# Products of zeros on TensorE through the whole routing, in counts per step

## The reference, cut to what matters

```
x = x + 0.5 * ffn(layernorm(x))
x = x + attention(layernorm(x))        # 16 heads of 16, causal
x = x + 0.5 * ffn(layernorm(x))

ffn(x):
    logits = x @ gate_w + gate_b                     # 8 experts
    probs = softmax(logits, axis=1)                  # over the 4096 tokens
    vals, idx = top_k(probs, 2)                      # 2 experts for each token
    y = relu(relu(relu(x @ w1[e] + b1[e]) @ w2[e] + b2[e]) @ w3[e] + b3[e])
    v[e] = sum over tokens of y[e] * (probs of e where e was chosen, else 0)
    out[token] = sum of v[e] over its 2 chosen experts
```

## Time and profile before

| | us |
|---|---|
| median of 3 runs | 2117.75 |
| lowest and highest | 2114.55, 2118.36 |
| the profiled execution's own time | 2126.23 |
| its span, first to last instruction | 2124.5 |
| TensorE busy / VectorE busy / ScalarE busy | 2047.7 / 1817.7 / 1598.6 |
| mean granted clock of TensorE, as a share of full | 0.975 |

### The profile page before, as it was taken

How to read it: one execution, slowest core, us unless ns; L and a number is a source line. 1 busy time by engine, 2 the same in 40 slices (tenths; PEclk the granted TensorE clock), 3 DMA queues, 4 the chain that set the end, 5 groups by cost and what they waited for, 6 DMA issues and landing times.

```text
span 2124.5 us, 99858 instructions
## 1 busy us (share of the span) xinstructions
PE 2047.7 (96%) x43659; PEld 1584.0 (75%) x43659; DVE 1817.7 (86%) x4023; ACT 1598.6 (75%) x3311; POOL 414.5 (20%) x1118
## 2 busy tenths in 40 slices
PE   5899989999999999999999999999999999879998
PEld 3788866377877777777787777777778776658885
DVE  6666666899999999999999999999999994676665
ACT  5344446599999999999999999999999998334442
POOL 1333213411121111121111111111111111023330
PEclk8899989999999999999999999999999999979998
DMA  8211103300010000100001001000010002231112
GB/s 273 74 47 50 42 16 125 134 30 25 13 34 14 25 30 8 34 20 18 31 7 33 22 16 34 9 29 27 11 34 16 22 4 69 54 118 47 45 49 88
DMA packets 70394, 94.36 MB, mean 44 GB/s; under 512 B 16640, under 2 KB 59396, under 8 KB 69956
## 3 DMA queue, kind: packets, MB, share of 16 engines
q1 hardware_dynamic: 62796, 68.75, 10.1%
q0 software_dynamic: 6816, 19.20, 3.4%
q10 hardware_dynamic: 344, 0.01, 0.0%
HBM read 62.24 MB, written 25.43 MB: 41 GB/s over the span
## 4 chain that ended last, share of the span: by engine, by line
PE 88%; DVE 6%; issue 2%; ACT 1%; POOL 1%; DMA 1%; SPq 1%; another core or an unknown queue 0%; DVEq 0%; ACTq 0%; POOLq 0%
PE bank L1264 39%; PE bank L1257 22%; PE bank L1139 17%; PE bank L1346 3%; PE bank L1150 1%; PE bank L1375 1%; DVE stats L1405 1%; PE bank L1307 1%; PE bank L1157 1%; DVE rows L1427 1%; DVE x_res L1725 1%; SPq L698 0%; POOL work L591 0%; DVE work L1594 0%; PE bank L1217 0%
## 5 line engine op out<-in xcount | busy, mean ns | idle before, releaser
L966 ACT ACTIVATE feat<-bank 128x512 f32<-128x512 f32 (+3 forms) x2304 | 1263.2, 565 | 113.8 <-PE bank L1264 13.3
L1264 PE MATMUL bank<-work 96*32 96x512 bf16 (+2 forms) x15872 | 1206.4, 370 | 5.0 <-DVE work L1772 3.8
L1772 DVE TENSOR_REDUCE work<-bank 128x1 f32<-128x512 f32 (+1 forms) x1920 | 1178.9, 659 | 26.4 <-PE bank L1264 23.4
L1257 PE MATMUL bank<-feat,phase 128*17 128x128 f32 (+3 forms) x18432 | 879.2, 263 | 0.3 <-ACT feat L972 0.3
L1257 PEld LDWEIGHTS bank<-feat,phase 128*17 128x17 f32 x18432 | 588.4, 98 | 270.7 <-ACT feat L972 13.7
L1264 PEld LDWEIGHTS bank<-work 96*32 96x32 bf16 (+1 forms) x15872 | 472.6, 96 | 57.1 <-DVE work L1772 24.6
L1139 PE MATMUL bank<-work 128*128 128x256 f32 (+1 forms) x1872 | 398.4, 363 | 0.6 <-issue 0.2
L1139 PEld LDWEIGHTS bank<-work 128*128 128x128 f32 x1872 | 325.1, 192 | 37.1 <-issue 1.0
L625 POOL TENSOR_SCALAR_AFFINE_SELECT feat<-feat 128x128 f32<-128x128 f32 x512 | 145.1, 292 | 456.0 <-ACT feat L966 439.1
L1656 DVE COPY work<-phase 128x514 f32 x234 | 101.5, 436 | 124.1 <-ACT work L880 99.5
L578 POOL DMA_INDIRECT work<-token_table,row_no x142 | 138.1, 973 | 299.0 <-PE bank L1150 142.6
(11 more groups left out here) (201 smaller groups left out, 1371.9 us busy)
## 6 DMA issues: line engine op xcount, KB each, us to landing
phase<-in_w SPq DMA_DIRECT2D x12, 1024.0 KB, 12.0
work<-qk_parts SPq DMA_DIRECT2D x60, 192.0 KB
token_table<-rows SPq DMA_DIRECT2D x8, 1056.0 KB, 8.7
work<-work SPq DMA_DIRECT2D x512, 0.5 KB
qk_parts<-phase SPq DMA_DIRECT2D x20, 384.0 KB, 2.8
work<-qk_parts SPq DMA_DIRECT2D x60, 128.0 KB
qk_parts<-work SPq DMA_DIRECT2D x12, 384.0 KB, 2.8
x_res<-in_x SPq DMA_DIRECT2D x8, 512.0 KB
```

What stands on the lines that cost most here:

```text
L966: eng.activation(p_ring[:, n % P_RING, lo:QB], s_bank("probs", n)[:, lo:QB], ACT.Exp, scale=HD ** -0.5).then_inc(sig.s_done, 1)
L1257: mm = eng.matmul(bank[ACC_BANK][GRID * g:GRID * g + VW, GRID * i0:P], v_aug[:, t, h, :], weights[:, i0:TPJ, g, :], start=(t == 0), stop=( ...
L1264: mm = eng.matmul(out[GRID * g:GRID * (g + 1), width], left[:, GRID * g:GRID * (g + 1)], right, start=start, stop=stop)
L1772: eng.tensor_reduce(maxima[:, h % 2, j, PLACE[i], at:at + 1], scores[:, 0:hi - lo], AX_X, ALU.max).then_inc(sig.a_done, 1)
```

## The change

A table gives the number of products of zeros for each step, and there are now some after the steps behind the counts, beside the first batch of one-hot columns (3 when its first instruction is done, 5 when its second is), and 3 ahead of each further batch of one-hot products. The five at the tiles' start stay as they were. The step `col_max` has none any more. Only TensorE's program is changed.

```diff
+BESIDE_CHOICE = {"pad": 2, "shifted": 6, "col_sum": 3, "inv_sum": 1, "probs": 2, "max_so_far0": 3, "from_top0": 2, "sel0": 2,
+                 "rest": 2, "max_so_far1": 3, "from_top1": 2, "sel1": 2}
+BESIDE_COUNTS = {"rounded": 1, "full": 1, "expert_rest": 1, "full_sum": 1, "over_half": 1, "left": 1, "others": 1}
+BESIDE_SLOTS = {"position": 2, "beyond": 2, "beyond_slots": 2, "slots": 2, "all_slots": 2, "my_slots": 3, "slots_of": 3,
+                "digits_hi": 1, "digits_lo": 1}
+BESIDE_HOTS = (3, 5)
+BETWEEN_HOTS = 3
...
+            def product_of_zeros():
+                eng.matmul(bank[4][:, :], zeros_bf[:, 0:P], zeros_bf[:, :], start=True, stop=True)
+
             def busy_beside(f, steps):
 
-                for name in steps:
+                for name, count in steps.items():
                     need.wait_ge(sig.routed[f], ROUTED[name])
-                    eng.matmul(bank[4][:, :], zeros_bf[:, 0:P], zeros_bf[:, :], start=True, stop=True)
+                    for _ in range(count):
+                        product_of_zeros()
 
             def route(f):
...
-                busy_beside(f, ROUTE[:ROUTE.index(FIRST_CHOSEN)])
+                busy_beside(f, BESIDE_CHOICE)
...
                 eng.matmul(bank[6][:, 0:NT * E], ones_bf[:, :], by_expert, start=True, stop=True).then_inc(sig.counted[f], 1)
+                busy_beside(f, BESIDE_COUNTS)
                 chosen_rows(f, 0, NT // 8)
+                busy_beside(f, BESIDE_SLOTS)
+                for made, count in enumerate(BESIDE_HOTS):
+                    need.wait_ge(sig.hots[f], made + 1)
+                    for _ in range(count):
+                        product_of_zeros()
                 for b in range(TOP * NT):
+                    if b and b % HOTS == 0:
+                        for _ in range(BETWEEN_HOTS):
+                            product_of_zeros()
                     need.wait_ge(sig.hots[f], 3 * (b // HOTS + 1))
...
             def tiles(f):
-                busy_beside(f, ["row_no"] * GATHER_FILL)
+                busy_beside(f, {"row_no": GATHER_FILL})
```

## The result

| | before | after |
|---|---|---|
| median, both on the same chip, 22 runs each (us) | 2117.53 (2113.92 to 2120.91) | 2120.67 (2118.80 to 2124.76) |
| the profiled execution, its span (us) | 2126.23, 2124.5 | 2121.85, 2120.1 |
| mean granted clock | 0.975 | 0.984 |

The ratio is 1.0018, 95% interval [1.0011, 1.0025]: by it the change is 3.8 us slower, where 2.3 us faster was forecast (the two medians as they stand are 3.1 us apart). 2120.67 lies just above the range. The clock did come up, and the kernel got slower.

What follows compares the result with a forecast made beforehand. It took VectorE's steps to bound the routings, with at most a few microseconds of 2117.75 hanging on TensorE's clock there. Gains of 1.17 us per routing, 2.3 in all, other terms 0, gave 2115.4 us; range 2112.0 to 2120.6.

Steps and rivals of the forecast that it cites:

- What bounds the kernel now: Routings' chain is mostly VectorE's; TensorE's clock matters at zeros, counts and last 16 one-hot products, at most a few microseconds.
- One-hot products: Last batch of each routing ends at 63.78 against 64.95 us: 1.17 us gained, with 0.5 from the counts.
- p: Time from one one-hot product to the next: 0.137 us at half clock, taken as 0.10 at full.
- Count products: Ahead of `running`: counts start 0.14 us later but shorten at full clock; gain 0.5 us, at worst a loss of 3.4.
- The loads do not quicken: Rival at the one-hot products: 0.137 us each even at full clock, +0.93 us x 2, 2119.6 us; chance 0.20.
- Does the clock stay up?: In the routings: full clock holds through the choice; a fall would mend itself as zeros queue at 0.43 us each.
- The clock falls among the one-hot products: Rival at 55 to 62 us: a batch takes 3.47 us, 2.9 us lost per routing, 2123.5 us; chance 0.10.
- Slots: Zeros behind the counts (7) and beside VectorE's slot steps (18): nothing on the chain waits, 0 us.
- Tiles' start: At the gather's wait the fill ends early, about 1 us idle; cost between 0 and 0.9 us, taken as 0.
- More is won at the tiles' start: Rival at the first tiles: both routings escape half clock costing up to 1.7 us, 2112.0 us; chance 0.12.
- Sum: Over both routings: 1.17 us gained in each, 2.3 us in all, giving 2115.4 us.

Runs made afterwards that it cites:

- e10: The changed kernel run again, unaltered: median 2129.76 us, ratio to before 1.0022.
- e5: Changed kernel without zeros between batches, plus six unused groups of 16 products per routing with weights and columns in steps of 16, 4 or 1; run once, 2144.41 us.
- e3: Kernel before with only the change's zeros in the choice, 30 ahead of the counts where 13 were: 2125.41 us, ratio 0.9994.
- e13: Kernel before with the chosen experts' columns stored by expert, so the count products read adjacent columns: 2116.84 us, ratio 1.0004.
- e1: Changed kernel without the 3 zeros ahead of each of one-hot batches 2 to 4: 2126.14 us, ratio to before 1.0005.
- e8: Changed kernel with one product of zeros between one-hot batches instead of 3: 2130.00 us, ratio to before 1.0019.
- e7: Changed kernel with all its zeros and the one-hot columns laid out in runs of 4: 2124.73 us, ratio to before 0.9994.
- e15: Kernel of e11 with the counts' columns stored as in e13 and all the change's zeros added: 2118.45 us, ratio to before 1.0012.
- e2: Kernel before plus only the 3 zeros ahead of each of one-hot batches 2 to 4: 2130.42 us, ratio 1.0017.
- e4: Kernel before with 8 products of zeros ahead of the last one-hot batch in each routing: 2131.13 us, ratio 1.0022.
- e12: Kernel of e11 with 27 zeros in the choice instead of 13: 2124.71 us, ratio to before 1.0002.
- e9: The kernel before, unaltered, run once more for its profile: 2121.63 us.
- e11: Kernel before with one-hot columns in runs of 4 and VectorE's `tile_mask` moved behind `row_no`: 2121.88 us, ratio 0.9988.

## Why the prediction was wrong

**What bounds the kernel now** held as to the places: in a routing of before the chain passes through TensorE at the zeros ahead of the counts, the counts, and the last 16 one-hot products. But I took the duration of both kinds of product to be a matter of the clock, without a row at full clock for either.

**One-hot products** is the step that failed, and it decided the sign. I took p = 0.10 us, between bounds of 0.069 and 0.137; it was 0.135 to 0.136 (after and e10 at full clock), at the upper bound. At this p the prediction's own sum gives 2.84 us a batch (measured 2.82 to 2.83) and a loss: the rival "The loads do not quicken". Its price of 0.93 us a routing had 0.5 us of gain at the counts in it; without that gain it is 1.4, and e10's first routing lost 1.7. The cause that I gave for p, the weight loads, was wrong (e5): weights in steps of 16 alone come every 0.061 us. The moving columns, 71 of them, set it. What misled me was that the load rows stood in the same cadence (149 ns each); a load that waits for the product ahead of it would show that cadence too (this reading is argued, and e5 only agrees with it).

**Count products** failed too. The 0.14 us of later start was right to the hundredth (e3, e10: 1.72 against 1.58), the gain of 0.5 was not there: 0.43 us apart at full clock as at half. I had read these 0.43 us as the price of 256 columns at half clock; they are the price of a step of 16 bytes (e13). The loss bound there, a queue of half-speed zeros ahead of the counts, came in part: 0.6 to 1.0 us in six routings in which the clock fell at the choice's start (after twice, e1, e3, e8 and e10 once each), 0.3 or less in three more (e5, e7, e15).

**Does the clock stay up?** Not through the choice, where I took it to hold: it fell at 36.6 and 1852.5 us. It was back at full by 40.0 and 1855.9 us, so that fall mended itself, as said, and through the slots the clock held. Among the one-hot products no: it fell at 60.5 and 1876.4 us, after stretches in which TensorE's record is full. That is the rival "The clock falls among the one-hot products", put at 0.10; its batch of 3.47 us was 3.42 (after) and 3.45 (e2), and its loss of 2.9 us a routing was 3.1 and 3.3, counts included. That these lie so close is in part luck: the rival's sum has a gain of 0.5 us at the counts in it, where 0.9 and 0.6 us were lost, and a fall ahead of all three gaps, where the first gap still ran at full clock. So two rivals came true together. The reason against it ("the zeros between, and a queue full until 55 us") was worth nothing: a full queue was there when the clock fell.

**Slots** cost nothing, as said (e1: 20.50). With a fall there they cost about 1 us a routing, as e15 shows.

**Tiles' start.** The 0 was right for the kernel asked about: after has 19.61 and 19.34 us from the first tile to the sixth, e13, without the zeros, 19.69 and 19.33. The mechanism named there, a fill that ends early, about 1 us of idle and 0.9 us for a fall behind it, is real and rightly priced: e15 pays it, at 1.2 and 1.1 us. The changed kernel escaped it because its clock was at half anyway: its five zeros took 2.34 us and left no idle time. But the idle time of 2.53 us in the earlier trace rows was no property of the kernel. The rival built on it ("More is won at the tiles' start", 0.12) priced the half clock behind it, up to 1.7 us, about rightly (last section), but on the chip on which both kernels were timed there was most likely nothing of it to win.

**Sum.** In the profile of after the loss is 3.1 and 3.3 us a routing (`row_scaled` from `col_max`: 33.48 and 33.13, before 30.34 and 29.82). With e10's routings at 1.3 and 3.7 by the same measure, the mean of four is 2.85 a routing, 5.7 in all; timed, by the ratios, were 3.8 and, in e10's group, 4.7 us. The profiled executions of after, e2, e4 and e10 are each 1 to 3.5 us above their kernels' medians. Of the unprofiled executions only the mean granted clock is on record. Its median is a little above the profiled one for after (0.985 against 0.984), e2 (0.975 against 0.972) and e10 (0.985 against 0.984) and equal for e4 (0.976), and within each of these kernels the slower executions tend to be those with the lower clock. So fewer stretches at half clock are likely a part of it; where they fell is not on record, and the rest stays open.

## What to carry to other kernels

Before you credit a product with a faster clock, look at how its operands lie: a product whose moving columns are read in steps of 16 bytes or more took the same time at both clocks, and only its layout made it faster. Filling a gap of a queue with work of no use has to be priced at half clock: here 26 to 30 of them ran in one piece through a fall and delayed what stood behind them (after, e15), and three in a gap took 1.28 us and not 0.65. Ahead of something on the chain that cost more than the clock brought. And where the bounds of an unknown lie on both sides of the sign, measure that one size, or give the bad end its due.

## What the runs showed of the hardware

**The step of the moving columns.** At 32 bytes 1.82 ns a column, at 16 bytes 1.7 (0.43 us for 256), at either clock; at 8 bytes 0.96 at full clock and 0.97 at half; side by side 0.45 and 0.83. VectorE paid for a step as well: 256 numbers of bf16 written in steps of 64 bytes took 1.27 us, not 0.42.

**Signals of TensorE that come late.** In most products the reader of a result starts 0.04 us after the last product's end. In every profile of e1 to e12 (chips 4, 13 and 3), and in the profile of before above, two groups of the first tiles of each routing are read late, by 0.7 to 4 us and mostly by 2 to 4; in the profile of after, and in those of e13 to e15 (chip 7), none is. VectorE and ScalarE in before, behind products that ended at 73.7 and 75.4 us (a wait that the profile can put down to no instruction of the core's other engines is called "issue" or "remote"):

```profile
76.55 0.61 DVE L1689 TENSOR_SCALAR work<-bank,work 128x128 f32<-128x128 f32 x2 [3.12 <-issue]
...
78.77 0.84 ACT L880 ACTIVATE work<-bank,work 128x256 f32<-128x256 f32 x2 [5.53 <-remote]
```

The same two places in after, and in e10, which is the same program:

```profile
77.30 0.61 DVE L1711 TENSOR_SCALAR work<-bank,work 128x128 f32<-128x128 f32 x2
...
79.03 0.84 ACT L889 ACTIVATE work<-bank,work 128x256 f32<-128x256 f32 x2 [2.24 <-PE bank L1161]
```

```profile
77.64 0.61 DVE L1711 TENSOR_SCALAR work<-bank,work 128x128 f32<-128x128 f32 x2 [2.47 <-remote]
...
80.53 0.84 ACT L889 ACTIVATE work<-bank,work 128x256 f32<-128x256 f32 x2 [5.56 <-remote]
```

In before, TensorE's semaphore updates then come in a burst, 34 ns apart, from 78.74 us. From the first tile to the sixth it is 24.0 and 23.4 us with this and 19.6 and 19.3 without, 8.5 us in a launch: near the 7.6 to 10.4 us by which the groups' medians of before differ (2116.52 against 2124 to 2127). It goes with the chip or the set of runs and not with the program (e9, e10).

The time from the first tile to the sixth also depends on the clock. In the profiles with late signals it is 22.4 to 22.6 us in the eight routings in which the clock stayed at full from the third tile to the sixth (both of e9, one each of e1, e3, e7, e8, e10 and e11), and 23.3 to 25.8 in the eighteen in which it did not. This differs between two profiles of one program: in before above it fell there in both routings, in e9 in neither. So the times of e1 to e12 carry some us that belong to no edit; the distances from mark to mark do not.

What holds the signals back was not found. What it teaches is plain: idle time with "issue" or "remote" beside it, ahead of an engine whose work had long been done, is not to be put down to the kernel until a profile of it from another chip has it too.
